# Attention and low-rank expert layer on one core: router product moved among the warm-up products, and one quarter of q moved ahead of the first scores

## What is computed

```python
def _L0_xattn_ref(query, key, value, position_ids, Wq, Wk, Wv, Wo):
    q = einsum('bse,ef->bsf', query, Wq); k, v = ...   # by heads of 16
    q = q * cos + _rotate_half(q) * sin
    k = k * cos + _rotate_half(k) * sin
    scores = einsum('bhqd,bhkd->bhqk', q, k) * scale
    ctx = einsum('bhqk,bhkd->bhqd', softmax(scores), v)
    return einsum('bsf,fe->bse', ctx, Wo)

def _L0_ffn_ref(x, A_w, B_w, Wq_w, keys):
    q = einsum('bsd,rd->bsr', x, Wq_w)
    scores = einsum('bsr,er->bse', q, keys)
    top_vals, top_idx = top_k(scores, 16)
    gate = ...                          # softmax of the 16, zero elsewhere
    z = einsum('bsd,nd->bsn', x, A_w)   # 64 experts x 8
    return einsum('bsn,on->bso', z * gate, B_w) * 2.0

x = x + _L0_xattn_ref(_layernorm(x), ctx_4096, ctx_4096, positions, Wq, Wk, Wv, Wo)
x = x + _L0_ffn_ref(_layernorm(x), A_w, B_w, Wq_w, keys)
```

## Time and profile before

| | us |
|---|---|
| median of 3 runs | 175.37 |
| lowest and highest | 175.06, 175.51 |
| profiled execution | 174.97 |
| its span, first to last instruction | 173.3 |
| PE busy | 167.6 (97%) |
| DVE busy | 132.6 (77%) |
| ACT busy | 90.3 (52%) |
| POOL busy | 85.2 (49%) |

### The profile page before, as it was taken

One profiled execution on the slowest core, in us unless ns is written; L12 is line 12 of the kernel. 1 busy time (PEld: TensorE's weight loads), 2 busy tenths in 40 slices (PEclk: granted clock), 3 DMA queues, 4 the chain that ended last, 5 costly groups with the idle time before them and its releaser, 6 DMA issues.

```text
span 173.3 us, 4057 instructions
## 1 busy us (share of the span) xinstructions
PE 167.6 (97%) x1440; PEld 130.9 (76%) x1440; DVE 132.6 (77%) x391; ACT 90.3 (52%) x206; POOL 85.2 (49%) x109
## 2 busy tenths in 40 slices
PE   7999999999989999999999999999999999999994
PEld 2656674577869887888879887888879776889883
DVE  1758857987999899849996699549984998758651
ACT  3478899756468335652837344752528345334210
POOL 5499989599569926423581326402550302422100
PEclk9999999999999999999999999999999999999999
DMA  5999912002102020101001000100001001000013
GB/s 150 319 402 384 407 48 62 0 6 61 62 2 61 4 61 0 62 4 34 29 4 61 0 4 0 64 2 0 4 0 61 4 0 61 4 4 0 0 61 121
DMA packets 5331, 11.30 MB, mean 65 GB/s; under 512 B 688, under 2 KB 944, under 8 KB 5056
## 3 DMA queue, kind: packets, MB, share of 16 engines
q1 hardware_dynamic: 5024, 10.79, 17.9%
q10 hardware_dynamic: 288, 0.27, 0.4%
HBM read 8.95 MB, written 2.10 MB: 64 GB/s over the span
## 4 chain that ended last, share of the span: by engine, by line
PE 86%; DVE 7%; ACT 3%; issue 2%; ACTq 0%; DVEq 0%
PE ps_w L1053 13%; PE ps_w L1054 12%; PE ps_w L1058 12%; PE ps_t L1066 9%; PE ps_s L1113 6%; PE ps_s L1149 5%; PE ps_s L1132 4%; PE ps_w L1206 3%; PE ps_w L1214 3%; PE ps_t L1071 3%; PE ps_w L1046 3%; PE ps_w L1047 3%; PE ps_w L1048 3%; PE ps_s L1054 2%; PE ps_s L1053 2%
## 5 line engine op out<-in xcount | busy, mean ns | idle before, releaser
L313 POOL TENSOR_TENSOR oT_lo<-o_n,oT_hi 128x512 fp32r<-128x512 f32 x8 | 10.3, 1291 | 30.5 <-ACT oT_hi L507 30.5
L771 DVE TENSOR_REDUCE ps_s<-ps_s 128x8 f32<-128x512 f32 x32 | 21.0, 692 | 0.9 <-PE ps_s L1113 0.7
L499 ACT ACTIVATE eT<-ps_s 128x512 f32<-128x512 f32 x32 | 17.0, 600 | 4.1 <-PE ps_s L1138 4.0
L328 POOL TENSOR_TENSOR late<-late,gate 128x512 f32<-128x512 f32 x7 | 7.6, 1081 | 19.7 <-DVE gate L864 19.7
L1053 PE MATMUL ps_w<-am_hi,x2T_hi 128*128 128x288 f32 x48 | 13.9, 312 | 0.0
L1054 PE MATMUL ps_w<-am_lo,x2T_hi 128*128 128x288 f32 x48 | 13.1, 296 | 0.0
L304 POOL TENSOR_TENSOR k_bd_lo<-kT_lo,half_mask 128x512 fp32r<-128x512 f32 x8 | 8.8, 1096 | 7.7 <-DVE kT_lo L743 7.7
L1214 PE MATMUL ps_w<-wq_sb,xT_raw 128*128 128x512 f32 x24 | 11.8, 606 | 0.0
L1053 PE MATMUL ps_w<-wo_hi,oT_hi 128*128 128x512 f32 x28 | 11.3, 405 | 0.4 <-ACT oT_hi L507 0.4
L789 DVE STREAM_TRANSPOSE o_s<-ps_s 128x1024 f32<-128x1024 f32 x8 | 9.9, 1243 | 1.8 <-PE ps_s L1149 1.8
L507 ACT ACTIVATE oT_hi<-o_n 128x512 fp32r<-128x512 f32 x8 | 5.1, 632 | 12.0 <-DVE o_n L804 12.0
(11 more groups left out here) (211 smaller groups left out, 524.9 us busy)
## 6 DMA issues: line engine op xcount, KB each, us to landing
x_sb<-x SPq DMA_DIRECT2D x8, 256.0 KB, 6.9
cT_in<-cT SPq DMA_DIRECT2D x7, 256.0 KB, 3.7
out<-res SPq DMA_DIRECT2D x7, 256.0 KB, 2.0
wq_sb<-wq SPq DMA_DIRECT2D x4, 256.0 KB, 6.2
late<-wo SPq DMA_DIRECT2D x1, 1024.0 KB, 8.2
am_sb<-aT SPq DMA_DIRECT2D x1, 1024.0 KB, 8.4
b_sb<-bT SPq DMA_DIRECT2D x1, 1024.0 KB, 7.0
wkv_sb<-wkv SPq DMA_DIRECT2D x1, 512.0 KB, 4.7
```

Of the source, the lines that this page charges most:

```text
L313: pool.tensor_tensor(oT_lo[:], o_n[:].rearrange("p (b r q) -> p r b q", b=2, r=REP), oT_hi[:].bitcast(F32), ALU.subtract).then_inc(oT_lo_o ...
L499: act.activation(eT[:, c].rearrange("p b n -> p (b n)"), ps_s[:, c, :], ACT.Exp)\
L771: dve.tensor_reduce(neg_top[:, b, HALF_H * half:HALF_H * (half + 1), :], ps_s[:, 2 * (1 - b) + half, :].rearrange("p (r h k) -> p h r k", ...
```

## The change

- The load of the router matrices is taken from SP's queue, where it stood between x(1) and wo, and put first on ACT's queue, ahead of pos and cT(0).
- WARM goes from 12 to 7. The four router products follow the seven, ahead of turn_xh(0), with their wait for ld_router; they are taken from between turn_q(0) and raw_q(1, 0).
- ACT's copy of ROUTE into am_sb goes from behind values_out(1) to right behind the first table load, ahead of the wait for wkv.
- raw_q(1, 1) goes from behind turn_k(1) to behind raw_q(1, 0), ahead of scores(0, 0).

```diff
-WARM = 12
+WARM = 7
@@ block.sync
             load_x(1)
-            sp.dma_start(router_sb[:], router).then_inc(ld_router, 16)
             sp.dma_start(wo_sb, wo).then_inc(ld_wo, 16)
@@ block.scalar
+            act.dma_start(router_sb[:], router).then_inc(ld_router, 16)
             act.dma_start(pos_sb[:], pos).then_inc(ld_pos, 16)
             act.dma_start(cT_in[:, 0], cT[0]).then_inc(ld_c[0], 16)
@@ ACT first()
                 act.activation(preload[:, 0:1], half_pi[:], ACT.Sin)
+                act.wait_ge(route_ps, 1)
+                act.activation(am_sb[:, :, 0:E], ROUTE.rearrange("p (k e) -> p k e", k=DK), ACT.Copy)\
+                   .then_inc(route_ok, 1)
                 act.wait_ge(ld_wkv, 16)
...
                 values_out(1)
-                act.wait_ge(route_ps, 1)
-                act.activation(am_sb[:, :, 0:E], ROUTE.rearrange("p (k e) -> p k e", k=DK), ACT.Copy)\
-                   .then_inc(route_ok, 1)
                 act.wait_ge(ld_wo, 16)
@@ PE first()
                 keep_warm(ps_t1[:], WARM)
+                pe.wait_ge(ld_router, 16)
+                for k in range(DK):
+                    mm = pe.matmul(ROUTE[:, E * k:E * (k + 1)], router_sb[:, P * k:P * (k + 1)],
+                                   router_sb[:, D:D + E], start=True, stop=True)
+                mm.then_inc(route_ps, 1)
                 pe.wait_ge(ident_ok, 1)
...
                 turn_q(0)
-                pe.wait_ge(ld_router, 16)
-                for k in range(DK):
-                    mm = pe.matmul(ROUTE[:, E * k:E * (k + 1)], router_sb[:, P * k:P * (k + 1)],
-                                   router_sb[:, D:D + E], start=True, stop=True)
-                mm.then_inc(route_ps, 1)
                 raw_q(1, 0)
+                raw_q(1, 1)
                 scores(0, 0)
                 pe.wait_ge(route_ok, 1)
                 scores(0, 1)
                 turn_k(1)
-                raw_q(1, 1)
                 raw_q(1, 2)
```

## The result

The changed kernel takes 177.84 us in the median (177.12 to 178.85, 6 runs), against 175.12 for the kernel before in the same set (175.06 to 175.51, 6 runs). The ratio is 1.0156, with a 95% interval of 1.0125 to 1.0188: 2.7 us slower. Forecast were 176.0 and at most 177.5. The profiled execution took 177.95 us, with a span of 176.2.

A forecast was written before the change was run, and what follows sets the result against it. PE's queue of work bounds the kernel from turned_scores(0) at 23.15 us, so its start sets the end. Late pos 0.55 plus 0.05 for raw_q(1, 1) gives 0.6: 175.37 + 0.6 = 176.0 us, range 175.2 to 177.5.

The forecast's parts named there:

- The direction and the place: Start of the kernel: a later pos on ACT's queue delays xh(0), shift, scores and turned_scores(0), 0.6 us slower.
- the size of pos's delay: ACT's queue: pos is issued one router issue later and so lands 0.55 us later, moving DVE's first work.
- cT(0) was called hidden: ACT's queue: cT(0) lands at 6.6 us, still ahead of raw_kv(0) at 7.07, so its delay costs nothing.
- The clock rival: PE's start: thinner warm-up raises the clock late; raw_kv(0) at 1.2 GHz gives 177.5, half of it 176.7; chance 0.28.
- Path 2: From pos over abs_r, POOL's splits, shift and ACT to x_raw(1): moves by the whole 0.55 us and gates the scores.
- path 1: From pos over xh(0) to PE: turn_xh(0) starts at about 6.8 us instead of 6.36, moving PE's path by 0.45.
- raw_q(1, 1) fills what the router product leaves: Ahead of scores(0): raw_q(1, 1) takes up the freed 1.03 us, scores start at 17.68 against 17.69; +0.05 us taken.
- Router product into the warm-up: Behind seven warm-up products: router product takes 1.03 to 2.06 us, ending between 5.3 and 6.3, ahead of xh(0).
- The range: Median time of the changed kernel: 175.2 to 177.5 us, taking in no change and most of the clock's case.

The follow-up runs named there:

- e1: Kernel before with only the router's transfer moved, first on ACT's queue ahead of pos and cT(0); 177.53 us, ratio 1.011.
- e5: Kernel before with ACT waiting before issuing pos, so pos goes out at about 1.23 us with no router ahead of it; 175.65 us, ratio 1.0023.
- e7: Changed kernel with DVE doing the statistics of x(0) and xh(0) ahead of the copy of pos; 178.03 us, ratio 1.0145.
- e11: Kernel before with the router's transfer second on ACT's queue, between pos and cT(0); 176.88 us, ratio 1.009.
- e13: Kernel of e1 with WARM = 18 instead of 12; ratio 1.0097, six runs from 176.38 to 177.89 us.
- e4: Changed kernel with raw_q(1, 1) back behind turn_k(1); 177.85 us.
- e8: Changed kernel with WARM = 12 instead of 7; four runs from 177.23 to 177.54 us, ratio 1.011.
- e6: Changed kernel with the router's transfer second on SP's queue, behind x(0), and raw_q(1, 1) back behind turn_k(1); 175.99 us, ratio 1.0031.
- e14: Kernel of e6 with WARM = 9 instead of 7; 175.42 us, ratio 1.0002.
- e15: Kernel of e14 with x(1) issued ahead of cT(1) on SP's queue; 176.21 us, ratio 1.0012.
- e2: Kernel before with WARM = 7 instead of 12 and nothing else; 175.35 us, ratio 1.0008.
- e9: Kernel of e4 with the router's transfer issued first by POOL on a queue of its own and WARM = 8; 177.38 us, ratio 1.0111.
- e10: Kernel of e9 with raw_q(1, 1) ahead of scores(0, 0); 176.86 us, ratio 1.0101.
- e3: Changed kernel with pos and cT(0) issued ahead of the router on ACT's queue; 179.16 us, ratio 1.0201.
- e12: Kernel before with cT(0) first on ACT's queue and pos behind it, held back until POOL's half_mask is made; 182.57 us, ratio 1.0406.

## Why the prediction was wrong

**The direction and the place** were right: slower, through pos on ACT's queue. xh(0), shift and the scores came late in that order, and what is behind turned_scores(0) passed the delay on.

**The step that failed is the size of pos's delay.** "On ACT's queue pos is issued later by one issue", so 0.55 us, took the landing to move with the issue. pos landed 1.58 us later; e1 gives 1.5 with that edit alone, worth 1.4 us of span, and e5 gives nothing for the same issue time without the router ahead. A number that spoke against the step was at hand in the trace of before, beside cT(0)'s 4.9 us:

```profile
eT<-router SPq DMA_DIRECT2D x1, 36.0 KB, 6.4
```

The router's 36 KB took 6.4 us to land from their place on SP's queue, so a landing depends on what is ahead and beside, and the length of an issue is no price for it. In the Trainium skill, "DMA: Bandwidth & Descriptors", Queues, rings and completion order, each DMA engine takes turns between the queues that have work, a packet at a time, and takes up the work of one queue in order. The 2.7 us of the router at the head of ACT's queue and the 5.9 us in third place agree with it. Which packets pos stood behind was not looked at, so this mechanism is argued, not shown; that the router ahead of it is the cause is shown by e1 with e5.

**cT(0) was called hidden.** "It lands at 0.78 + 0.40 + 4.9 + 0.55 = 6.6": it landed at 8.5, by the same error: a landing that was taken to move with the issue. What made it late is less clear than for pos, since e5's profile has it at 9.0 without the router. In the changed kernel the late xh(0) covers it; in e7 and e11, where xh(0) is early, it costs PE 1.19 and 1.30 us.

**The clock rival was priced right and stood as an alternative to the late pos, when the two add up.** It put raw_kv(0) at the lower level at 1.73 us; the trace has 1.68, and 0.26 more in the first three quarters of q. It got a chance of 0.28. The runs show two ways to it. One is the late pos, with twelve warm-up products and none of the thin ones ahead: five of e1's seven runs pay, and one of six when more products fill the wait (e13); in e4 and e8 the granted value shows the fall to 0.50 around PE's idle time. The other is the shorter warm-up with the router product behind it, and pos in time: five of ten (e6), four of twelve (e14), seven of twelve (e15) are slow. e6's profile still lost the level around 1.00 us of idle time, but in e15's there is none, and it is what the rival said: a level that rises late. e2, with seven products and no thin ones, has four of ten, so whether the thin products add anything to the shorter warm-up isn't told apart. With both together, all six runs of the change pay: the lowest span is 175.4, where e1's good runs have 174.7. The profiled one is of the second kind, slow from the first product on.

In spans, the change loses 2.9 us: 1.4 are pos's (e1's good runs), 1.1 are what e13 buys back of e1, and the 0.4 left over were not taken apart; the order of raw_q is among them.

**Path 2 against path 1.** The prediction let POOL's path carry the whole delay and PE's only 0.45 us. At the full clock that is so: in e1's profile PE waited for xh(1), and the whole delay came through. In the changed kernel ACT waited 1.00 us for PE ahead of x_raw(1), and POOL 0.32 us for DVE: PE's path, with its slow passes, came last. The step held, and was overtaken by the clock.

**raw_q(1, 1) fills what the router product leaves.** Predicted: the scores no earlier, PE idle 0.86 us ahead of turn_m(0), nothing gained. Measured: 0.84 us idle, and scores that start 3.35 us late, behind a raw_kv(0) that ends 3.43 late. e9 against e10 says that leaving raw_q(1, 1) in its place gains 0.48 at the scores and 0.1 to 0.2 at the end. Right in the main; that about 0.3 us come back further on was not foreseen.

**Router product into the warm-up.** It took 1.97 us (foreseen: 1.03 to 2.06) and ended ahead of xh(0); ACT's copy and the splits of wkv cost nothing. Right as a cost of time; its part in the late clock is open.

**The range** ended at 177.5 because it took the clock's case with a pos that is 0.45 us late. With the measured 1.5 in its place it would have ended near 178.6.

## What to carry to other kernels

A load in the first microseconds is not priced by its issue: for every load that is moved back on a queue, read the time to landing of loads in that place, and look who waits. Work taken out of a full stretch of one engine is worth the slack of the next engine in line (here 0.2 us of 1.03 at the scores), and is dear if its operand pushes back what the first real work waits for. Warm-up products should last until that work starts, at whichever pace they run: here the slow start that often follows an idle gap cost 1.1 us and more, beside 1.4 for the delay that made the gap. And a warm-up that is cut short can cost the same with no gap at all.

## What the runs showed of the hardware

- A transfer of 36 KB took 2.5 to 2.8 us from issue to landing at the head of ACT's queue, 3.4 in second place behind 4 KB and 5.9 in third; in second place on SP's queue, behind 256 KB, it took 2.7 to 2.8 (e6, e14, e15). One of 4 KB took 2.6 to 3.2 us at the head, 4.0 to 4.3 behind the 36 KB, and 6.4 behind 256 KB and issued at 2.8 us. Issued 0.45 us later with nothing ahead, it landed no later.
- cT(0), 256 KB on ACT's queue, took 3.2 to 3.3 us when wkv (512 KB, SP's queue) was issued 0.5 us behind it (e6, e14, e15), 4.8 to 4.9 when wkv was issued at the same time (before, e2, e3, e9, e10), and 6.2 to 7.4 when wkv was 0.4 to 0.5 us ahead (the change, e1, e4, e5, e7, e8, e11, e13). In the last group the router stands ahead of cT(0) as well, except in e5.
- PE, idle for 1.5 us (e8) or 2.4 us (e4) behind its warm-up, went from 2.4 to 1.2 GHz (granted 1.00 to 0.50), in e8 at 7.7 us, while still idle, and in e4 at 8.3, in its first real work. It stayed there for 3.4 us in both, and for 6.8 us in the profiles of e3, e5 and e12. With 1.85 us of idle time e1's profile kept the full level (8 passes of raw_kv(0) in 1.73 us), and five of its seven runs paid; with 0.35 us (e13), one of six.
- The lower level can last from the first product into the real work with no idle time between: in e15's profile until after 11.4 us, with a granted value of 1.00 throughout.
- Whether the level rises within the warm-up differs between executions: twelve products took 5.1 us in one (1.24 to 6.36) and 4.2 us in another (1.24 to 5.41, e8).
